# Second attention of a two-layer block: scores two batches ahead, last projection and routing placed earlier, pads sent when counts are known

## The reference

```
xn = layernorm(x)
s  = attention0(xn)                 # 16 heads of 64, q/k of unit length, two null keys, linear bias, causal
g  = silu(experts0(xn))             # 8 experts, the best one per token, gelu, 128 -> 512 -> 128
x  = x + s * g
xn = layernorm(x)
s  = attention1(xn)                 # one head of 128, causal, out = layernorm(att @ v + v) @ Wfc + bfc
g  = silu(experts1(xn))             # 8 experts, the best two per token, capacity 2*2*T/8 rows each
x  = x + s * g
```

## Time and profile before

| | |
|---|---|
| median of 3 runs | 1137.81 us (1132.39 to 1138.07) |
| profiled execution | 1137.35 us, its span 1135.5 us |
| TensorE busy | 1012.4 us (89%), mean granted clock 0.951 |
| VectorE, ScalarE, POOL busy | 686.7, 659.4, 668.5 us |
| DMA | 103.70 MB, 91 GB/s on the mean |
| chain that ended last | PE 55%, DVE 14%, issue 12%, ACT 8% |

### The profile page before, as it was taken

How to read it: one execution, slowest core, us unless ns; L and a number is a source line. 1 busy time by engine, 2 the same in 40 slices (tenths; PEclk the granted TensorE clock), 3 DMA queues, 4 the chain that set the end, 5 groups by cost and what they waited for, 6 DMA issues and landing times.

```text
span 1135.5 us, 22426 instructions
## 1 busy us (share of the span) xinstructions
PE 1012.4 (89%) x6668; PEld 745.6 (66%) x6668; DVE 686.7 (60%) x2553; ACT 659.4 (58%) x1973; POOL 668.5 (59%) x821
## 2 busy tenths in 40 slices
PE   5798999999999999899999998998889978999950
PEld 2675566666668996566666665666568857989840
DVE  6737876776763336776776777867654353345326
ACT  4635667667755557667666666675554434544434
POOL 3425588788854555677676687887345422545443
PEclk9678999999999999999999999999999889999985
DMA  9200112202526742203302122032131044777745
GB/s 293 63 5 1 26 37 63 68 24 64 151 47 197 221 147 62 55 25 70 64 7 60 28 57 65 25 76 53 31 83 29 29 140 142 211 209 224 216 134 149
DMA packets 97385, 103.70 MB, mean 91 GB/s; under 512 B 10447, under 2 KB 85238, under 8 KB 97040
## 3 DMA queue, kind: packets, MB, share of 16 engines
q1 hardware_dynamic: 90256, 89.96, 30.2%
q0 software_dynamic: 7040, 12.66, 3.2%
HBM read 77.29 MB, written 25.28 MB: 90 GB/s over the span
## 4 chain that ended last, share of the span: by engine, by line
PE 55%; DVE 14%; issue 12%; ACT 8%; POOL 4%; DMA 3%; SPq 2%; another core or an unknown queue 1%; POOLq 0%; DVEq 0%; ACTq 0%
PE bank L1138 11%; PE bank L641 8%; PE bank L630 8%; PE bank L1167 7%; PE bank L1194 5%; PE bank L1182 4%; PE bank L1157 4%; DVE arena L1731 4%; PE bank L1219 3%; ACT arena L1479 3%; POOL arena L906 2%; DVE arena L1740 2%; ACT arena L1468 1%; PE bank L1071 1%; ACT XN L355 1%
## 5 line engine op out<-in xcount | busy, mean ns | idle before, releaser
L1479 ACT ACTIVATE arena<-arena 128x128 f32<-128x128 f32 (+1 forms) x512 | 226.9, 446 | 118.9 <-DVE arena L1731 118.4
L1731 DVE CUSTOM_DVE_ANT_0 arena<-bank,arena 128x128 f32<-128x128 f32 (+1 forms) x512 | 182.9, 413 | 141.1 <-PE bank L1167 134.8
L906 POOL TENSOR_TENSOR arena<-arena 128x512 f32<-128x512 f32 x128 | 132.7, 1042 | 164.4 <-ACT arena L1455 157.0
L1138 PE MATMUL bank<-arena 128*128 128x512 f32 x384 | 210.3, 637 | 15.5 <-ACT arena L1468 11.7
L1740 DVE COPY arena<-bank 128x384 f32<-128x384 f32 x256 | 130.3, 549 | 24.3 <-PE bank L1182 20.3
L604 POOL DMA_INDIRECT expert_out<-arena x78 | 77.0, 987 | 101.6 <-DVE arena L710 86.1
L921 POOL TENSOR_TENSOR arena<-arena 128x512 f32<-128x512 f32 x128 | 129.9, 1049 | 1.3
L1182 PEld LDWEIGHTS bank<-const,arena 128*128 128x128 f32 x768 | 91.7, 142 | 56.2 <-issue 56.0
L1455 ACT ACTIVATE arena<-bank 128x512 f32<-128x512 f32 x192 | 112.6, 587 | 26.9 <-PE bank L1138 26.7
L1167 PE MATMUL bank<-arena 64*128 64x128 f32 (+1 forms) x1024 | 120.0, 353 | 8.4 <-DVE arena L1731 5.5
L1194 PE MATMUL bank<-arena 128*64 128x256 f32 (+1 forms) x1024 | 111.8, 339 | 6.9 <-DVE arena L1740 6.3
(11 more groups left out here) (277 smaller groups left out, 1806.1 us busy)
## 6 DMA issues: line engine op xcount, KB each, us to landing
arena<-in_wp SPq DMA_DIRECT2D x39, 514.0 KB
arena<-recip_rows SPq DMA_DIRECT2D x30, 512.0 KB, 6.2
XN<-in_wp SPq DMA_DIRECT2D x23, 514.0 KB
arena<-expert_rows SPq DMA_DIRECT2D x62, 129.0 KB
arena<-expert_out SPq DMA_DIRECT2D x16, 256.0 KB, 5.4
arena<-in_b SPq DMA_DIRECT2D x62, 64.0 KB
expert_out<-fill SPq DMA_DIRECT2D x11, 338.6 KB, 7.6
expert_rows<-fill SPq DMA_DIRECT2D x1, 2967.0 KB, 22.5
```

The lines of the kernel that those rows point to most:

```text
L906: pool.tensor_tensor(sq[:, i % 2], r, r, ALU.mult).then_inc(S["sq_done"], 1)
L1138: mm = pe.matmul(RING[bnk][:, :], xa[:, p, t * P:(t + 1) * P], wqkv[:, 512 * k:512 * k + 512], start=True, stop=True)
L1479: ins = act.activation(w, w, ACT.Exp, bias=nm[:, p, 16 * t + h:16 * t + h + 1], scale=-1.0, accum_out=den[:, p, 16 * t + h:16 * t + h + 1])
L1731: ins = v.tensor_tensor_reduce(out=SPb[:, c % 2, 384 * k + P * t:384 * k + P * t + n], in0=SBANK[k][:, P * t:P * t + n], in1=alibi[:, h, N ...
```

## The change

- **Scores two ahead.** SC becomes two banks, 3 and 4, taken in turns. `scores1(0)` and `scores1(1)` run ahead of the first step, and a step computes `scores1(b + 2)` at its end, behind `zv1(b + 2)` and `weigh1(b - 1)`. It waits for the maximum of b (`ttr1_done >= b + 1`). VectorE's order becomes `rows_max1(b + 1)`, routing work, `residual(b - 1)` in one flat list.
- **Bank Y2 goes.** Both halves of the last projection use MISC, one tile before and one behind TensorE's `step1(1)`; ranks of group 3 use RT instead of MISC.
- **Last pair of batches.** POOL scales the last batch's outputs ahead of `send_rows(2, 1)`. `y_out`, `norm_rows`, `second_layer_norm`, `turn_last(10)`, `logits_last(10)`, `ranks1(5)` and the masks each stand one to three steps earlier. `send_rows(3, 1)` comes before `send_rows(4, 0)`.
- **Pads.** `held` counts up `pads_ready` right with the cast of the counts. SP waits for it first, sends the eight pads, then waits for the owners and loads the weights.
- **Folding.** `fold_weights` moves into `step(6)`, behind its sixth pair of heads.

No instruction of work is added or removed. The diff, without the new semaphore's name, the index `[p]` on SC in `rows_max1`, and `y_out`'s argument:

```diff
@@ -474,7 +474,7 @@
     v.wait_ge(S["rank_evac"], 1 + len(GROUPS))
-    v.tensor_copy(padtab, RUN[0:1, 0:E])
+    v.tensor_copy(padtab, RUN[0:1, 0:E]).then_inc(S["pads_ready"], 1)
     link(v.tensor_scalar(CEN, cc(C_JJ, E), float(SPAN), float(CENTRE), ALU.mult, ALU.add))
@@ -571,20 +571,22 @@
         load_weights(j + NBUF, q)
-    sp.wait_ge(S["owner_ready"], layer + 1)
     if layer:
+        sp.wait_ge(S["pads_ready"], 1)
+        for e in range(E):
+            row = sp.value_load(padtab[0:1, e:e + 1], min_val=0, max_val=NOROWS)
+            sp.dma_start(xe[1][bass.ds(row, BLK), :].rearrange("(p r) d -> p (r d)", p=P), fill[:, :]).then_inc(S["filled"], 16)
         sp.wait_ge(S["ttr_done"], NB * 16)
+        sp.wait_ge(S["owner_ready"], 2)
         for j in range(NBUF):
 ...
         sp.wait_ge(S["tables_ready"], 1)
-        for e in range(E):
-            row = sp.value_load(padtab[0:1, e:e + 1], min_val=0, max_val=NOROWS)
-            sp.dma_start(xe[1][bass.ds(row, BLK), :].rearrange("(p r) d -> p (r d)", p=P), fill[:, :]).then_inc(S["filled"], 16)
         sp.wait_ge(S["scattered"], scattered)
 ...
     else:
+        sp.wait_ge(S["owner_ready"], 1)
         sp.wait_ge(S["scattered"], scattered)
@@ -1035,15 +1037,15 @@
     norm_root(len(SETS) - 2)
+    scale_out(NB - 1, 1)
+    last_ids()
     send_rows(2, 1)
-    last_ids()
-    scale_out(NB - 1, 1)
     send_rows(3, 0)
 ...
     norm_root(len(SETS) - 1)
+    send_rows(3, 1)
     send_rows(4, 0)
-    send_rows(3, 1)
     send_rows(4, 1)
@@ -1207,16 +1209,16 @@
         mm.then_inc(S["comb_full"], 1)
-    def project(b, p, t, half, out=MISC):
+    def project(b, p, t, half):
         if half == 0:
             pe.wait_ge(S["comb_evac"], b + 1)
-            if t and out is MISC:
+            if t:
                 pe.wait_ge(S["y_evac"], b * 2 + 1)
-            pe.matmul(out[:, 0:D], cT[0:2 * H, t * P:(t + 1) * P], nvw, start=True, stop=False)
+            pe.matmul(MISC[:, 0:D], cT[0:2 * H, t * P:(t + 1) * P], nvw, start=True, stop=False)
         pe.wait_ge(S["o_scaled"], b * 4 + (2 * half + 2))
         for c in range(4 * half, 4 * half + 4):
-            mm = pe.matmul(out[:, 0:D], OT[p][:, c, t * P:(t + 1) * P], wo0[:, c], start=False, stop=(c == HC - 1))
+            mm = pe.matmul(MISC[:, 0:D], OT[p][:, c, t * P:(t + 1) * P], wo0[:, c], start=False, stop=(c == HC - 1))
         if half:
@@ -1316,7 +1318,7 @@
     finish(NB - 1, 1)
-    ZB, VB, OB1, SC, Y2, RT, PT = bank[0], bank[1], bank[2], bank[3], bank[4], bank[5], bank[7]
+    ZB, VB, OB1, SC, RT, PT = bank[0], bank[1], bank[2], bank[3:5], bank[5], bank[7]
     def zv1(b):
@@ -1336,8 +1338,10 @@
         pe.wait_ge(S["z1_evac"], b + 1)
-        pe.matmul(SC[:, 0:P], z1[:, p, 0:P], x[:, 0:P], start=True, stop=True)
-        pe.matmul(SC[:, P:P + N], z1[:, p, P:N], x, start=True, stop=True).then_inc(S["s1_full"], 1)
+        if b >= 2:
+            pe.wait_ge(S["ttr1_done"], b - 1)
+        pe.matmul(SC[p][:, 0:P], z1[:, p, 0:P], x[:, 0:P], start=True, stop=True)
+        pe.matmul(SC[p][:, P:P + N], z1[:, p, P:N], x, start=True, stop=True).then_inc(S["s1_full"], 1)
     def weigh1(b):
@@ -1352,9 +1356,6 @@
         p = b % 2
-        if b + 1 < NB:
-            pe.wait_ge(S["ttr1_done"], b + 1)
-            scores1(b + 1)
         pe.wait_ge(S["exp1_done"], b + 1)
@@ -1365,6 +1366,8 @@
             weigh1(b - 1)
+        if b + 2 < NB:
+            scores1(b + 2)
     def turn_last(m):
@@ -1384,31 +1387,32 @@
     scores1(0)
+    scores1(1)
     step1(0)
-    ranks1(3, MISC)
+    pe.wait_ge(S["lg_evac"], 1)
+    ranks1(3, RT)
+    for half in range(2):
+        project(NB - 1, 1, 0, half)
     step1(1)
-    pe.wait_ge(S["lg_evac"], 1)
+    for half in range(2):
+        project(NB - 1, 1, 1, half)
+    pe.wait_ge(S["rank_evac"], 5)
     turn_last(9)
-    pe.wait_ge(S["rank_evac"], 5)
-    project(NB - 1, 1, 0, 0)
-    project(NB - 1, 1, 1, 0, Y2)
     step1(2)
     logits_last(9)
-    project(NB - 1, 1, 0, 1)
-    project(NB - 1, 1, 1, 1, Y2)
     step1(3)
     step1(4)
+    pe.wait_ge(S["lg_evac"], 2)
+    turn_last(10)
     pe.wait_ge(S["y_evac"], 2 * NB)
 ...
     step1(5)
-    pe.wait_ge(S["lg_evac"], 2)
-    turn_last(10)
+    logits_last(10)
     step1(6)
-    logits_last(10)
     step1(7)
-    step1(8)
     pe.wait_ge(S["rank_evac"], 6)
     ranks1(5, MISC)
+    step1(8)
     for b in range(9, NB):
@@ -1604,12 +1608,12 @@
     step1(3)
+    second_layer_norm(len(SETS) - 1)
     step1(4)
-    second_layer_norm(len(SETS) - 1)
+    turn_last(10)
     step1(5)
-    turn_last(10)
+    logits_last(10)
     step1(6)
-    logits_last(10)
     last_copy()
@@ -1819,6 +1823,8 @@
                 norm_rows(x1 - 1)
+            if isinstance(b, int) and b == FB + 1 and c == 5:
+                fold_weights()
             if x1 and b in RANK_STEP and c < 2:
@@ -1850,13 +1856,11 @@
     for b in range(FB + 1, NB):
-        if b == FB + 2:
-            fold_weights()
         step(b, b % 2, more=min(2, NB - 1 - b), flushed=b == FB + 1, x1=b - FB - 1)
     comb_out(NB - 1)
-    OB1, SC, Y2 = bank[2], bank[3], bank[4]
+    OB1, SC, RT = bank[2], bank[3:5], bank[5]
     SCL = float(D) ** -0.5
@@ -1919,40 +1923,50 @@
         mask_part(v, link, 3, k)
-    step1(0)
-    positions(v, link, 3, MISC)
-    step1(1)
-    step1(2)
-    for t in range(2):
-        y_out(NB - 1, t, (MISC, Y2)[t])
-    step1(3)
+    rows_max1(1)
+    positions(v, link, 3, RT)
+    rows_max1(2)
+    y_out(NB - 1, 0)
+    residual(0)
+    rows_max1(3)
+    y_out(NB - 1, 1)
+    residual(1)
+    rows_max1(4)
+    norm_rows(len(SETS) - 1)
+    residual(2)
     v.wait_ge(S["lg_evac"], 2)
-    for k in range(3):
+    for k in range(2):
         mask_part(v, link, 4, k)
-    norm_rows(len(SETS) - 1)
-    step1(4)
-    for k in range(3, 5):
+    rows_max1(5)
+    for k in range(2, 5):
         mask_part(v, link, 4, k)
-    step1(5)
+    residual(3)
+    rows_max1(6)
     positions(v, link, 4, MISC)
-    step1(6)
-    step1(7)
+    residual(4)
+    rows_max1(7)
     v.wait_ge(S["lg_evac"], 3)
 ...
         mask_part(v, link, 5, k)
-    step1(8)
+    residual(5)
+    rows_max1(8)
     for k in range(3, 5):
         mask_part(v, link, 5, k)
-    step1(9)
+    residual(6)
+    rows_max1(9)
     positions(v, link, 5, MISC)
     held(v, link)
-    step1(10)
+    residual(7)
+    rows_max1(10)
     tables(v, link, 0)
-    step1(11)
+    residual(8)
+    rows_max1(11)
     tables(v, link, 1)
-    step1(12)
+    residual(9)
+    rows_max1(12)
     gate_powers(v, link)
-    for b in range(13, NB):
+    residual(10)
+    for b in range(12, NB):
         step1(b)
```

More of the change, by code:

```diff
@@ L267, in block_kernel @@
             *[f"y1_in{q}" for q in range(8)], "second_scaled", "first", "tables_ready", "turned1", "mixed", "silu_done", "mixed_in", "l1w_in", "l1w_ready", "z1_full", "z1_evac", "v1_full", "v1_evac", "s1_full", "ttr1_done", "exp1_done", "pt1_full",
-            "pt1_evac", "o1_full", "rd1_done", "rd_layer1", "o1_done", "attn1_done", "copied", "first3", "copy_ids", "recip_half0", "recip_half1", "gate_exp", "out_ready", "out_done", "wexp")}
+            "pt1_evac", "o1_full", "rd1_done", "rd_layer1", "o1_done", "attn1_done", "copied", "pads_ready", "first3", "copy_ids", "recip_half0", "recip_half1", "gate_exp", "out_ready", "out_done", "wexp")}
         class Chain:
@@ L1772, in fold_weights, with y_out @@
                 v.tensor_scalar(wturn[:, 3], wv1, T2[:, 0:1], None, ALU.subtract).then_inc(S["l1w_ready"], 1)
-            def y_out(b, t, src=MISC):
+            def y_out(b, t):
                 v.wait_ge(S["y_full"], b * 2 + (t + 1))
-                v.tensor_scalar(RS_[:, bass.ds(b * 2 + t, 1), :].rearrange("p t d -> p (t d)"), src[:, 0:D], 0.5, None,
+                v.tensor_scalar(RS_[:, bass.ds(b * 2 + t, 1), :].rearrange("p t d -> p (t d)"), MISC[:, 0:D], 0.5, None,
                                 ALU.mult).then_inc(S["y_evac"], 1)
@@ L1866, in rows_max1 @@
                     v.wait_ge(S["exp1_done"], b - 1)
-                v.tensor_tensor_reduce(out=s1b[:, p, 0:P], in0=SC[:, 0:P], in1=mask1[:, P:2 * P], scale=-SCL,
+                v.tensor_tensor_reduce(out=s1b[:, p, 0:P], in0=SC[p][:, 0:P], in1=mask1[:, P:2 * P], scale=-SCL,
                                        scalar=-NEG, op0=ALU.add, op1=ALU.min, accum_out=nm1[:, 2 * p:2 * p + 1])
-                v.tensor_tensor_reduce(out=s1b[:, p, P:P + N], in0=SC[:, P:P + N], in1=mask1[:, :], scale=-SCL,
+                v.tensor_tensor_reduce(out=s1b[:, p, P:P + N], in0=SC[p][:, P:P + N], in1=mask1[:, :], scale=-SCL,
                                        scalar=-NEG, op0=ALU.add, op1=ALU.min, accum_out=nm1[:, 2 * p + 1:2 * p + 2])\
```

## The result

| | before | after |
|---|---|---|
| median of 20 runs each | 1137.84 us | 1131.39 us (1122.10 to 1137.09) |
| ratio | | 0.9941, 95% interval 0.9922 to 0.9959 |
| profiled execution | 1137.35 us | 1128.53 us, span 1126.7 us |
| from the first z matmuls of the second attention to the expert layer's first turn | 845.94 to 939.40, 93.5 us | 841.72 to 930.03, 88.3 us |
| TensorE busy in that stretch, granted clock | 78.78 us, 0.91 | 73.37 us, 0.96 |

The gain is 6.4 us where 13.6 was forecast: faster, and just inside the range's slow end. The profiled pair differs by 8.85 us of span. Of these, 2.4 us lie ahead of the first expert layer's end (424.48 and 422.05), where nothing was changed; 1.8 between it and the second attention; 5.2 in the second attention; 0.4 between the first turn and the first upward matmul; and 0.9 are lost again in the expert layer.

A forecast was written before the change was run, and what follows sets the result against it. Bound: second attention on TensorE and SP's pads ahead of the rows, ending together. Won 16.4 us by order after new waits, less 4.3 of stall, plus 1.5 for folding: 13.6 off 1137.35, so 1123.7 us; range 1117.5 to 1131.5.

The forecast's parts named there:

- the main term: Second attention: TensorE's idle times (10.5 us) and lowered clock (7.3 us more), together 17.8 us to be won by order alone.
- The scaled halves: Last batch's scaling on POOL, moved ahead of sends: halves at 854 and 856.5, 3 us earlier; TensorE waits for nothing.
- 1 us past the stretch that I had named: Sign of being right: the first block's matmuls in the second expert layer stand between 924 and 930 us.
- The wait at batch 6: Second attention: scores two ahead wait for ScalarE's z copy behind the last norm; cost 1.7 us, between 0 and 3.3.
- 16.4 us: Second attention's gain before any stall: 17.8, 0.5 at the layer's start and 0.3 in the tail, less 0.5 and 1.7.
- The stall that may stay: VectorE and ScalarE idle just after the first weights are issued; of 6.8 us, 4.3 given back.
- the stall stays away: Rival: no stall near the weight loads, as code positions move against the loads; 4.3 us more, 1119.4 us; chance 0.2.
- the second bound: SP's pads ahead of the expert layer's rows; TensorE close behind, so shortening SP's queue alone gains about 0.5 us.
- The waits of 1.59 and 2.10 us [...] go: Second attention: TensorE's waits on a z copy behind a late maximum vanish through scores two ahead on two banks.
- ScalarE did not become the bound: Rival: second attention's spare of 0.2 us lost by another 0.4 in twelve steps, stall returns fully; 1131.0 us; chance 0.18.
- the 152 that I had set as a limit: Sign of being wrong: a second expert layer longer than 152 us.
- Slower: Rival: pads and weights beside six unrolled steps bring four fetch stalls of 6.8 us; 1146.7 us; chance 0.04.

The follow-up runs named there:

- the order alone: Kernel after with scores one batch ahead, pads back behind weights and tables, folding in its old place; 1107.35 us, ratio 0.9856, again 1108.08 us, 0.9879.
- the second run of the kernel with all sends cut: Kernel after with POOL's row sends in the second attention cut into fours by waits until earlier sends landed; 1111.82 us, ratio 0.9902.

## Why the prediction missed

**Right.** The mechanism of the main term. Removing the gaps in front of the counts brings the clock back: it is 1.00 from 877 to 892, and no idle time stands in front of either count. Over the whole stretch that I had named, 877 to 902, it is 0.94 and not 0.97: the last 10 us hold the stall. The scaled halves, the projection and the norm gave TensorE no wait of note. The pads went out at 892.37 (said: 894.3) ahead of the weights, and the chain entered the expert layer by VectorE and TensorE, without a pad or a row in it; the first block's matmuls stand at 931.03, 1 us past the stretch that I had named. The wait at batch 6, "1.7 us there, between 0 and 3.3", was 0.27 in the first trace and 0.39, 1.20 and 2.57 in the three of the kernel after without the stall. Sum of the stage without stall: the prediction took 16.4 us off 93.5, which is 77.1; the kernel after has 77.2, 80.9 and 77.9. That it comes so near is in part luck, since two of its terms were wrong (below).

**The step that failed** is "The stall that may stay": "Between 0 and 6.8 us given back I take 4.3, nearer to what was there." In the measured pair the stage shrank by 5.2 us and not by 12.1. With 16.4 won by order, 11.2 were given back and not 4.3; against the three profiles of the kernel after without the stall it is 7.4 to 11.1. Idle time shows it: TensorE was idle for 14.7 us of the stage before (93.5 less 78.78) and for 14.9 after (88.3 less 73.37); 5.4 us of low clock were won and kept, and all idle time that was won went into the stall. The upper bound of 6.8 assumed that a stall can't be longer than the one seen. It can: 9.13 us on VectorE where 5.09 was, and another before it, of 3.28 and 3.35 us, at 862.01 and 865.73.

Its cause was misread as well. The prediction put a fetch of code behind the loads of 514 KB. The stall ended before these loads began, six of the seven stalls have no packet of code in them, and with the same 42 fetches of 0.69 MB in the page, none of the eighteen later profiles has a wait marked remote. For the rival "the stall stays away" I had named the Trainium skill (Runtime: NRT & Kernel Launch, Instruction fetch mechanics), by which the cost of crossing a block of code is mostly hidden. The later profiles agree with it, and the rival's stage came out. In the five later calls, on four chips, the kernel before takes 1122.4 to 1124.0 us; in the three with the kernel after its gain is 15.0, 11.7 and 15.2 us by medians, where the rival had 17.9.

**Three errors that these runs show.** First, the base: what the stall had cost the kernel before was inside the 17.8 us. Without the 6.8 its stage would be 86.7 us; it is 88.4 and 89.7, and the gain there 8 to 12 us, not 16.4. The rest of the difference is the second bound: "about 0.5 us earlier and no more" held only while the stall delayed TensorE. Without it TensorE waited 3.3 to 3.6 us for rows, some 2.3 more than the 1.17 that stay anyway. In the old order the early pads win that. In the new order the counts are ready so much earlier that late pads do as well: the stage is 77.3 us with them, 76.5 in the order alone. Second, "The waits of 1.59 and 2.10 us [...] go" was credited to the scores two ahead. With scores two ahead and the old order, 1.50 and 0.92 are still there; with one ahead and the new order, neither is. The order does it. That it is VectorE's taking a maximum before routing work and residuals fits, but is not tested by itself. Third, the expert layer was taken as a fixed length. With the folding alone it takes 153.0 us from its first turn to its last matmul, TensorE busy for 150.5 at 0.98, since it begins behind the wait of 3.58 us with the clock at 0.50 for 4 us; the kernel after takes 148.9 to 150.1 at 1.00 without the stall. So 3 to 4 us of the 12 to 15 lie there, outside the stage.

**Rivals.** ScalarE did not become the bound: in the kernel after without the stall TensorE waits over 0.3 us for a z copy in front of the scores of batches 2 and 6 alone, and with scores one ahead, where it has no such wait, the stage is shorter by 1 us or so. The expert layer took 153.2 us (152.3 before), a little over the 152 that I had set as a limit, and cannot carry the miss. "Slower" was built on stalls that multiply beside pads and weights. The stalls did grow, but beside the pads and in front of the weights.

**What stays open.** What causes the stall, and why it was longer in the new order. It belongs to the first measurement: in its chip or its time, which I can't separate. There both kernels are slower than in every later call, the kernel before by 14 to 15 us and the kernel after by 21 to 24, so the kernel after does suffer more from it there, and I can't say by which part of it. Only a part of this lies in the stage. From the end of the first expert layer's last matmul to the second attention the kernel before took 421.2 us there and 413.5 to 415.1 in the three later profiles with its order, the kernel after 419.4 against 409.7 to 414.4; and in the second expert layer the kernel after's TensorE was idle for 5.0 us, against 1.7 to 2.3. Both kernels had stalls in stage 3.

## What to carry to other kernels

Put the work that the next engine waits for (here the row maxima, and the routing ahead of the counts) in front of everything that has slack on the same engine, before spending a bank on distance: the order alone made the whole gain that a chip without the stall shows. An idle time marked remote in one profile is not a property of the kernel until a second measurement, on another chip, shows it; look for more of them in the whole trace, keep them out of the base, and don't bound what one may cost by the one that was seen. When a bound is removed, read how far behind the next queue stands, and read it without the stall: the pads were priced at 0.5 us with it, alone they won some 3 without it, and in the new order nothing that can be seen.

## What the runs showed of the hardware

Three engines can slow down at once with no cause that the trace names. For 12 us VectorE and ScalarE stood nearly still and SP took 2.0 us for each pad instead of 1.0, while POOL's sends kept their 1.28 us. Three later profiles of the same program have none of it, and sixteen sends back to back in another kernel, with the DMA engines busy for 0.73, cost TensorE nothing. And a gap of one size does not always bring the clock down: the wait of 2.57 us at batch 6 stood in a stage at 0.96, whose 400 matmuls took 73.8 us, and the clock was 0.74 from 867 to 880; in the second run of the kernel with all sends cut the same wait was 2.57 us too, the clock stayed at 1.00 and 400 matmuls took 70.7.
